# Recurrence as two chains over two PSUM banks, shorter LayerNorm pieces and a new order of products in a fused recurrent and gated block

## What is computed

```python
def _L0_attn_ref(x, W_in, b_in, W_out, b_out, gamma, beta):
    u = jnp.einsum('bsd,hd->bsh', x, W_in) + b_in          # 512 -> 1024
    def step(state, u_t):
        s = jnp.tanh(u_t + state * gamma + beta)
        return (s, s)
    _, states = jax.lax.scan(step, init, jnp.swapaxes(u, 0, 1))
    return jnp.einsum('bsh,dh->bsd', jnp.swapaxes(states, 0, 1), W_out) + b_out

x = x + _layernorm(_L0_attn_ref(_layernorm(x), ...))
x = x + _layernorm(_L0_ffn_ref(_layernorm(x), ...))
# _L0_ffn_ref: (silu((x @ gate_q) * gate_scale) * ((x @ up_q) * up_scale)) @ down_q * down_scale
# gate_q, up_q: 512 x 1536, down_q: 1536 x 512, all rounded to float8_e4m3fn
```

## Time and profile before

| what | value |
|---|---|
| median of 3 runs | 586.48 us (586.11 to 586.82) |
| span of the profiled execution, first to last instruction | 584.4 us |
| rest of a run around the span (median less span; the profiled execution has no time of its own on record) | 2.1 us |
| busy: PE, DVE, ACT, POOL | 554.9, 394.4, 331.3, 205.4 us |
| mean granted TensorE clock | 0.990 |
| the chain that ended last, by engine | DVE 48%, ACT 22%, PE 21%, issue 6%, POOL 2% |
| first scan of the recurrence, last scan (starts) | 18.08 us, 522.11 us |

### The profile page before, as it was taken

One profiled execution on the slowest core, in us unless ns is written; L12 is line 12 of the kernel. 1 busy time (PEld: TensorE's weight loads), 2 busy tenths in 40 slices (PEclk: granted clock), 3 DMA queues, 4 the chain that ended last, 5 costly groups with the idle time before them and its releaser, 6 DMA issues.

```text
span 584.4 us, 10121 instructions
## 1 busy us (share of the span) xinstructions
PE 554.9 (95%) x2984; PEld 464.7 (80%) x2984; DVE 394.4 (67%) x1639; ACT 331.3 (57%) x1516; POOL 205.4 (35%) x339
## 2 busy tenths in 40 slices
PE   8999899998999999999999999999999998998993
PEld 5767667988788978897898978898888787876992
DVE  3689899986686668575776668575767577746113
ACT  3687687845575546655575556654675455541330
POOL 1214316543153413632262323431243133522622
PEclk9999999999999999999999999999999998999998
DMA  7878379700101001200110000200020000200100
GB/s 259 274 225 239 72 210 203 148 1 1 37 18 56 1 0 39 73 0 2 36 61 14 0 6 33 72 2 0 2 74 0 1 2 0 73 1 1 37 0 37
DMA packets 20055, 33.78 MB, mean 58 GB/s; under 512 B 2720, under 2 KB 4896, under 8 KB 20000
## 3 DMA queue, kind: packets, MB, share of 16 engines
q1 hardware_dynamic: 16544, 26.84, 13.8%
q0 software_dynamic: 3456, 6.29, 6.1%
HBM read 22.63 MB, written 4.19 MB: 46 GB/s over the span
## 4 chain that ended last, share of the span: by engine, by line
DVE 48%; ACT 22%; PE 21%; issue 6%; POOL 2%; DMA 1%; SPq 0%; POOLq 0%; DVEq 0%; ACTq 0%
DVE recur L1014 22%; ACT pairs L1302 13%; PE gate_up L933 7%; PE wide L868 6%; DVE fused L1137 6%; PE wide L890 4%; DVE peaks L1201 3%; ACT gated L1325 3%; ACT fused_hi L1341 3%; ACT pairs L1289 2%; DVE powers L1184 2%; PE wide L956 2%; DVE x_norm L1107 2%; DVE y L1054 2%; DVE rounders L1191 2%
## 5 line engine op out<-in xcount | busy, mean ns | idle before, releaser
L1014 DVE TENSOR_TENSOR_SCAN recur<-recur,pairs 128x32 f32<-128x32 f32 x1024 | 236.0, 230 | 137.8 <-ACT pairs L1302 134.2
L1302 ACT ACTIVATE pairs<-recur 128x16 f32<-128x16 f32 x1024 | 191.3, 187 | 191.6 <-DVE recur L1014 186.4
L1424 POOL TENSOR_TENSOR fused_lo<-fused,fused_hi 128x256 fp32r<-128x256 f32 x96 | 72.0, 750 | 137.7 <-ACT fused_hi L1341 137.6
L890 PE MATMUL wide<-w_out_sb,pairs 128*128 128x512 f32 x256 | 114.4, 600 | 4.7 <-ACT pairs L1302 4.7
L933 PE MATMUL gate_up<-x_hi,gate_q 128*128 128x256 f32 x384 | 103.3, 301 | 4.3 <-DVE x_lo L1122 4.3
L868 PE MATMUL wide<-x_norm_t,w_in_sb 128*128 128x256 f32 x448 | 100.8, 381 | 4.6 <-ACT x_norm_t L1257 2.5
L890 PEld LDWEIGHTS wide<-w_out_sb,pairs 128*128 128x128 f32 x256 | 74.6, 297 | 37.5 <-ACT pairs L1302 7.3
L868 PEld LDWEIGHTS wide<-x_norm_t,w_in_sb 128*128 128x128 f32 x448 | 84.0, 190 | 19.2 <-ACT x_norm_t L1257 4.8
L933 PE MATMUL gate_up<-x_lo,up_q 128*128 128x256 f32 x384 | 97.0, 285 | 0.0
L933 PE MATMUL gate_up<-x_hi,up_q 128*128 128x256 f32 x384 | 96.7, 284 | 0.0
L933 PE MATMUL gate_up<-x_lo,gate_q 128*128 128x256 f32 x384 | 96.5, 284 | 0.0
(11 more groups left out here) (117 smaller groups left out, 567.4 us busy)
## 6 DMA issues: line engine op xcount, KB each, us to landing
x_in<-x SPq DMA_DIRECT2D x16, 256.0 KB, 3.4
x_res<-x SPq DMA_DIRECT2D x16, 256.0 KB, 3.1
out<-z SPq DMA_DIRECT2D x14, 256.0 KB, 3.5
w_in_sb<-w_in_t SPq DMA_DIRECT2D x4, 512.0 KB, 6.2
w_out_sb<-w_out_t SPq DMA_DIRECT2D x8, 256.0 KB, 4.4
raw_own<-down_w SPq DMA_DIRECT2D x8, 256.0 KB, 2.9
raw_own<-rounders POOLq DMA_DIRECT2D x6, 256.0 KB, 4.6
raw_own<-gate_w SPq DMA_DIRECT2D x5, 256.0 KB, 4.3
```

The lines of the kernel that those rows point to most:

```text
L890: ins = eng.matmul(wide[b][:, :], pairs_by_batch[:, state_slots(n, b), :, j, 0].rearrange("p s b -> p (s b)"), w_out_sb[:, j, :], start=(j ...
L1014: eng.tensor_tensor_scan(preact.rearrange("p c k -> p (c k)"), factors.rearrange("p c k -> p (c k)"), pairs[:, (t - 1) % RING, :, :].rearr ...
L1302: eng.activation(pairs[:, t % RING, :, 0], preact[:, :, 1], ACT.Tanh).then_inc(s_state, 1)
L1424: eng.tensor_tensor(fused_lo[:, f, :], fused[:, f, :], fused_hi[:, f, :].bitcast(F32), ALU.subtract).then_inc(s_fused_lo, 1)
```

## The change

From block 2 on (`TWO_CHAINS_FROM = 2`, step 256) a step has two scans and two tanh instead of one each: one pair for each batch, with 16 elements in a scan and 8 in a tanh. Batch 0 stays in the bank of `recur`, batch 1 uses a bank of its own, `recur_second`. That bank is taken from the gated part, which now has two `gate_up` banks (`NG = 2`). y is copied, measured and normalized in four pieces of 128 columns from block 2 on, and so is x1 (both but for the last tile); x is measured in four from block 4 on; the product `fuse` is made in two pieces of 128 tokens for all blocks but the first and the last. z and the low part of x1 keep pieces of 256. The x transposes of blocks 4 to 7 go to the `wide` banks. PE's order is written out in the table `BETWEEN`, and the planner takes other engines' jobs as 5% longer in steps there. The matmuls are the same in number and size.

```diff
+FIRST_Y_AT_CHUNK = 4
+BETWEEN = {
+    1: {2: "y023", 9: "y1", 11: "x0 x1", 13: "u0", 14: "u1", 15: "u2 t0 u3 t1 Y001"},
...
+    5: {12: "t0", 13: "t1", 14: "Y001", 15: "Y023"},
+    6: {4: "y1", 12: "t0 t1"},
+}
...
+TWO_CHAINS_FROM = 2
+NG, NF = 2, 3
+PACE = 1.05
+def row_parts(kind, n, b, last):
+    if kind == "x":
+        return 4 if n >= TWO_CHAINS_FROM + 2 else 2
+    if kind in ("z", "low"):
+        return 2
+    return 2 if n < 2 or (n, b) == (last, 1) else 4
+def chunk_parts(p, last):
+    return 2 if 1 <= p < last else 1
...
+                if engine not in ("vector", "scalar") and self.two_chains_from <= now < self.last_step:
+                    steps *= PACE
...
-        NG = 3
+        recur_second = ps("recur_second", [P, 512])
+        second = recur_second[:, 0:4 * KH].rearrange("p (v c k) -> p v c k", v=2, k=2)
+        preact_of = [preact[:, 0:KH, :], second[:, 0, :, :]]
+        factors_of = [factors[:, 0:KH, :], second[:, 1, :, :]]
...
@@ vector: recurrence() @@
+                    if t >= SPLIT:
+                        for b in range(batch):
+                            columns = slice(b * KH, (b + 1) * KH)
...
+                            else:
+                                eng.wait_ge(s_state_of[b], t - SPLIT)
+                            eng.tensor_tensor_scan(preact_of[b].rearrange("p c k -> p (c k)"),
+                                                   factors_of[b].rearrange("p c k -> p (c k)"),
+                                                   pairs[:, (t - 1) % RING, columns, :].rearrange("p c k -> p (c k)"),
+                                                   0.0, ALU.mult, ALU.add).then_inc(s_preact_of[b], 1)
+                        continue
...
@@ scalar: recurrence() @@
+                    if t >= SPLIT:
+                        for b in range(batch):
+                            columns = slice(b * KH, (b + 1) * KH)
+                            eng.wait_ge(s_preact_of[b], t - SPLIT + 1)
+                            eng.activation(pairs[:, t % RING, columns, 0], preact_of[b][:, :, 1],
+                                           ACT.Tanh).then_inc(s_state_of[b], 1)
+                        continue
...
@@ tensor: gate_up_products() @@
-                        elif chunk >= NG:
-                            eng.wait_ge(s_fused, chunk - NG + 1)
...
+                        else:
+                            eng.wait_ge(s_fused, chunks_through(chunk - NG))
```

More of the change, by code:

```diff
@@ L198, in transpose_x @@
     def transpose_x(n, b, k):
-        t.tensor(("t1", n, b), TRANSPOSE_STEPS, [(("x_norm", n, b), 0.2)], k)
+        after = [(v, 0.2) for v in rows("y", "y_copy", n - 2, b)] if n >= 4 else []
+        if n == 3:
+            after = [(v, 0.2) for v in tokens("fuse", 0, KI - NG + b)]
+        t.tensor(("t1", n, b), TRANSPOSE_STEPS, [(("x_norm", n, b), 0.2)] + after, k)
         for h in range(2):
@@ L242, in gate_up @@
     def gate_up(p, i, after, k):
-        if KI * p + i >= 3:
-            after = after + [(("fuse", *divmod(KI * p + i - 3, KI)), 0.1)]
+        if KI * p + i >= NG:
+            after = after + [(v, 0.1) for v in tokens("fuse", *divmod(KI * p + i - NG, KI))]
         t.tensor(("gate_up", p, i), GATE_UP_STEPS, after, k)
+        read = [(("down", *divmod(KI * p + i - NF, KI)), 0.1)] if KI * p + i >= NF else []
         side("scalar", ("gate", p, i), [(("gate_up", p, i), BEHIND_TENSOR)], k)
-        side("vector", ("fuse", p, i), [(("gate", p, i), BEHIND_SIDE)], k)
@@ L248, in gate_up @@
-        before = [(("down", *divmod(KI * p + i - 3, KI)), 0.1)] if KI * p + i >= 3 else []
-        side("scalar", ("high", p, i), [(("fuse", p, i), BEHIND_SIDE)] + before, k)
+        for h in range(chunk_parts(p, LAST)):
+            side("vector", ("fuse", p, i, h), [(("gate", p, i), BEHIND_SIDE)], k)
+        side("scalar", ("high", p, i), [(v, BEHIND_SIDE) for v in tokens("fuse", p, i)] + read, k)
         side("gpsimd", ("low", p, i), [(("high", p, i), 0.1)], k, LOW_STEPS)
@@ L385, in timetable @@
+    lay_first(0, 2)
     for p in range(LAST):
         n = p + 2
-        if n <= LAST:
[L388 to L407, removed]
-                down(p, i - LAG, rank(n - 1, 7) + 0.1 * i, after=converted([GATE_UP_PIECES + i - LAG]) if p == 0 else ())
@@ L422, in timetable @@
-        for b in range(batch):
-            norm_z(p, b, ("down", p, KI - 1), rank(n, 30))
-    split_next(LAST, [batch - 1])
+        if p > 0:
+            if n + 1 <= LAST:
+                next_x(n + 1)
+            for i in range(KI + LAG + 1):
+                for item in BETWEEN[p].get(i, "").split():
+                    lay_between(p, item)
+                if i < KI:
+                    low = [(v, 0.2) for b in range(batch) for v in rows("low", "x1_low", p, b)] if i == 0 else []
+                    gate_up(p, i, low, rank(n - 1, 4.5) + 0.01 * i)
+                if LAG <= i < KI + LAG:
+                    down(p, i - LAG, rank(n - 1, 7 if i < KI else 9) + 0.1 * i)
@@ L425, in timetable @@
+        for b in range(batch):
+            norm_z(p, b, ("down", p, KI - 1), rank(n - 1, 20) if p > 0 else rank(n, 30),
+                   rank(n - 1, 5) if p > 0 else None)
+        if n <= LAST:
+            load(("x_res", n), [(("z_add", p, b), 0.2) for b in range(batch)], parts=batch)
     for i in range(KI):
-        low = [((*("x1_low", LAST, b), h), 0.2) for b in range(batch) for h in range(2)] if i == 0 else []
-        gate_up(LAST, i, low, rank(NB, 7) + 0.1 * i)
+        low = [(v, 0.2) for b in range(batch) for v in rows("low", "x1_low", LAST, b)] if i == 0 else []
@@ L428, in timetable @@
+        gate_up(LAST, i, low, rank(LAST, 4.5) + 0.01 * i)
         if i >= LAG:
@@ L433, in timetable @@
         norm_z(LAST, b, ("down", LAST, KI - 1), rank(NB, 10 + b))
+    last_piece = max(i for i in range(NP) if not by_transfer(i))
+    for h in range(2):
+        side("vector", ("second", h), [(v, 0.2) for v in pair("take", last_piece)], 90.0)
     t.jobs["down", 0, KI - 1].after.append((("guard", 3), 0.2))
```

306 lines of the change are left out of this document (199 added, 107 removed), and 3 rows, old and new, of the table BETWEEN.

## The result

| what | before | after |
|---|---|---|
| median of 4 runs each | 586.30 us (586.09 to 586.82) | 581.69 us (580.78 to 584.21) |
| ratio, 95% interval | | 0.9926 (0.9903 to 0.9948) |
| span and time of the profiled execution | 584.4, not on record | 579.0, 580.79 us |
| scan of step 256 to the last scan | 376.85 us | 355.67 us |
| last scan to the end of the span | 62.29 us | 77.85 us |

The forecast of no measurable change was wrong; its range held the time. The forecast gave faster a chance of 0.44. In the profiles of some experiments one step in block 0, long before the two chains, takes 3.25 instead of 1.56 us, since ACT waits longer for a u product of PE; that can be 1.7 of the 3.4 us between the fastest and the slowest of the new runs, and was not followed further.

What follows compares the result with a forecast made beforehand. Bound by the recurrence's latency, with PE nearly full: -16.4 us from the stretch and +15.8 behind it make -0.6 on a span of 584.4; with the median 2.1 above the span, 585.8 us, range 576.5 to 594.5.

Steps and rivals of the forecast that it cites:

- What bounds: Steps 256 on: recurrence within 2% of its own latency, PE busy 367.7 of 377.2 us, both nearly full.
- The free step: A step without extra work, from step 256 on: 0.4825 us falls by 0.039 to 0.443, 767 of them 339.8 us.
- The rival of the scan that does not shrink: Second scan starts 0.125 to 0.14 us after the first, steps with a piece grow: 596 to 608 us, chance 0.10.
- What PE gives back: Behind the last state: seven moved chunks add 19.9 us, less idleness and low clock take off 4.1, together +15.8.
- 4.1 of relief: Behind the last y product: seven chunks cover the LayerNorm that caused PE idleness and a lower clock, -4.1 us.
- What the second chain costs: Steps 256 to 1022: side pieces on DVE and ACT overrun the shorter step, sum 23.1 us, 19.6 after overlap.
- The waits: Waits of side pieces in the stretch from step 256: 1.0 us carried of the earlier 4.3, price from 0 to 8.
- The sum: Stretch 339.8 + 19.6 + 1.0 = 360.4 us, 16.4 earlier; with 15.8 given back, -0.6 on a span of 584.4.
- Side pieces that hide: Batches drift so ACT's pieces fall into the gap, silu and cast cost nothing (-8.9): 576 to 583 us, chance 0.32.
- Collisions with POOL: Pieces normalizing y and x1 are slowed while POOL subtracts, one in three by 0.26 us: 592 us, chance 0.16.
- Banks: Two banks stall gate_up over 2 us a block, within a rival of the order failing: 588 to 600 us, chance 0.06.
- The rule weighed against the change: PSUM sources cost 120 cycles + N: half fuse or y copy 0.26 us, 170 steps of 0.472, some 3 us more, 589.

Runs made afterwards that it cites:

- the kernel with wide pieces: Changed kernel with its short pieces undone, so all pieces are 256 wide as before, two chains and new order kept: 594.36 us, ratio 1.0128.
- the silu halves: Changed kernel with silu in two pieces of 128 tokens for blocks 1 to 6: 582.48 us, ratio 0.9925.
- the swapped kernel: Changed kernel with batch 1 ahead of batch 0 in each step on DVE and ACT: 580.77 us in 2 runs, ratio 0.9891.

## Why the prediction was half right

- **What bounds: right.** Recurrence by latency, PE behind it with little to spare.
- **The free step: right.** 0.443 forecast; rows of free steps have 0.4435 from scan to scan. The tanh's record fell by 8 ns (188 to 180), where the forecast had put 6 (8 columns at its own "at most 1.1 ns" would have been 9). The scan's record fell from 230 to 197 ns, 33 ns for 16 elements, the forecast's 2.2 ns each (0.033). The Trainium skill, page "DVE: opcode table, instruction layouts, handler registers and perf-mode slots", section "6. Datapath and trigger behaviour", says that this scan runs at half throughput; the trace agrees: at the 0.96 GHz that the Trainium skill's page "VectorE: DVE Perf Modes", section "Specifications", gives, 16 elements are then 33 ns by an estimate from these two pages. The rival of the scan that does not shrink falls.
- **What PE gives back: right.** +15.8 forecast, 77.85 - 62.29 = 15.6 measured, without a gap and at the full clock, as it said. Its 4.1 of relief was on the low side for this chain: with the last y product back at its old place the span is 6.3 longer.
- **What the second chain costs: the step that failed.** 19.6 and 1.0 of waits were forecast, 20.6 in all. 355.67 - 767 x 0.4435 leaves 15.5. Four prices were too high:

| piece | forecast over a free step | measured |
|---|---|---|
| half fuse (120 steps with nothing else) | 0.018 | 0.003 |
| 256 piece (54 steps) | 0.11 | 0.055 |
| silu, tanh to tanh | 0.10 | 0.07 |
| cast of `high`, tanh to tanh | 0.04 | 0.02 to 0.03 |

The cause has two parts. The sum let the second scan take as much of DVE as the first, 0.107, and set the second tanh as far behind the first; the trace has 0.08 for both. This 0.027 is all of the error for silu, and it is why the half fuse hides. And the 0.34 to 0.35 behind the y copy in the earlier trace rows was taken for the time that it fills. It is the distance to the next scan in a step of 0.49, which the latency sets as good as alone, so it is an upper bound only; with two scans in the step pieces of 256 columns fill 0.31 to 0.33. That two BN pieces one behind the other lie 0.34 apart is so, but with a scan behind it such a piece fills 0.32 in the kernel with wide pieces. The kernel with wide pieces bears out the measured prices: they made its stretch 14 longer, those of the prediction 20, and it was 13.3.

  Times the forecast's counts the four prices are 9 us too high (1.9 for half fuses, 4.3 for 256 pieces, 1.9 for silu, 0.9 for the cast), yet only 5.1 are missing. So some 4 us, by this estimate, were priced too low: steps with a 128 piece other than a fuse and nothing on ACT take 0.45 to 0.48 in the mean instead of 0.443, steps with a u copy 0.467 from tanh to tanh instead of 0.45, and the waits are longer. Two errors cancel in part here, which is luck.
- **The waits.** 1.0 forecast. One step holds more by itself, the 1.81 at 181.47 (1.4 over), behind an idle PE and the lower clock after it. The prediction had looked for the lower clock behind the last y, where it no longer falls.
- **The sum.** Forecast: a stretch of 360.4, 4.7 above the measured one. That is the whole miss on the span (583.8 against 579.0), since start and tail are within 0.25 us. With the margin of 1 ns a step that the prediction named itself, 5 us in one term decided whether a gain would be seen.
- **Rivals.** Side pieces that hide, 576 to 583: the time is theirs, the mechanism only in part, in full for half fuses and partly for the rest, and by another cause than a drift of the batches; silu and cast still lengthen their steps. Collisions with POOL: no. No piece of the stretch that normalizes y or x1 is recorded with more than 0.39 us (0.33 for those of 128 columns), where seven took 0.65 or 0.66 before; why none is hit now is open. Banks: PE waits 2.4 us for `fused` in three places, no more than 1.6 at once, so two banks are enough for this order; the silu halves show how near that is.
- **The rule weighed against the change.** The prediction had a step of 0.472 with a half fuse (589 us) by the rule of 120 cycles + N; such steps take 0.446. But it was the 0.214 for two scans that made 0.472. What a half fuse fills when no chain sets the pace shows behind the last state, two of them and the next piece in a row (timeline of DVE):

```profile
519.90 0.35 DVE L1297 SCALAR_TENSOR_TENSOR fused<-gate_up,up_scale_cols,gated 128x128 f32<-128x128 f32 x1 [1.25 <-ACT gated L1493]
520.17 0.34 DVE L1297 SCALAR_TENSOR_TENSOR fused<-gate_up,up_scale_cols,gated 128x128 f32<-128x128 f32 x1
520.43 0.42 DVE L1237 TENSOR_TENSOR x_res<-y,x_res 128x256 f32<-128x256 f32 x1
```

  There it fills 0.26 to 0.27; ahead of a scan no more than the 0.25 to 0.26 after which the scan starts. The Trainium skill, page "VectorE: DVE Perf Modes", section "The TRN2 errata", has 120 cycles + N at 0.96 GHz for a PSUM source, an estimate of 0.26 for 128 columns. The trace does not contradict that: with 0.107 and 0.08 for the two scans, 0.26 makes 0.447, against 0.446 measured. For 256 columns the same row gives 0.39, again an estimate: the whole fuse fills 0.37 to 0.38, but the y and z copies, which read PSUM too, 0.32 to 0.33, and there the trace disagrees.

## What to carry to other kernels

The distance from a piece to the next instruction of a chain is an upper bound of what the piece fills unless the chain waits for it; take prices from steps that the piece lengthens, and do not price a second instruction of a kind by the first. When two resources are both within 2 or 3% of full, value a faster one only together with the place where its last result is used: here the same chain was worth 0.7% with the last product right behind it and nothing with that product seven chunks later. And cutting pieces smaller shortens a step but lengthens the way of the work through the engine, so what is gained in steps can come back as a late matmul.

## What the runs showed of the hardware

- A scan that follows another of its kind is recorded with 174 ns against 197, and the next piece starts 0.08 us after it, the scan itself 0.11 after the first. It goes with the place in the row, as the swapped kernel shows.
- Two tanh of 8 columns start 0.07 to 0.08 us apart.
- Half a fuse (128 columns, read from PSUM) with the other half behind it fills 0.27 us of DVE, a whole one with a scan behind it 0.37 to 0.38, a y or z copy of 256 columns with a scan behind it 0.32 to 0.33.
- After 3.87 us without work PE was granted 0.63 of its clock over the next 4 us, and 0.94 over the 4 after that; after 5.05 us, 0.50, the lower of its two levels (1.2 of 2.4 GHz), and then 0.98. That costs 1.7 us (4 x 0.37 + 4 x 0.06) and 2.1 us, over 40% of the wait once more.
